# Attention over 64 keys: probabilities kept with the keys as rows, sums by TensorE, and keys and values made in the first layer

## What is computed

```python
x = x + per_token_matrix(layernorm(x), itok, ctx)      # row s is multiplied with a 256x256 matrix of ctx, chosen by itok[s]
x = x + top1_of_8_experts(layernorm(x), ...)            # 256 -> 512 -> 256, gelu
# third layer: q from layernorm(x), k and v from ctx, 16 heads of 16
scores = jnp.einsum('bhqd,bhkd->bhqk', q, k) * scale
scores = scores + mask * -1000000000.0
attn = jax.nn.softmax(scores, axis=-1)
ctx = jnp.einsum('bhqk,bhkd->bhqd', attn, v)
return jnp.einsum('bsd,ed->bse', ctx, Wo) + bo
x = x + gated_ffn_nvfp4(layernorm(x), ...)              # 256 -> 1024 -> 256, fake-quantized
```

## Time and profile before

| | |
|---|---|
| median of 3 runs | 788.87 us (785.74 to 792.18) |
| span of the profiled execution | 786.0 us |
| PE, DVE, ACT, POOL busy over the span | 78%, 74%, 51%, 27% |
| attention, 364 to 542 us: TensorE busy | 175.55 of 178 us |

### The profile page before, as it was taken

The page is one execution under the profiler, slowest core; times in us unless marked ns, Lnnn a source line. Parts: engine busy times, 40 slices in busy tenths (PEclk is TensorE's granted clock), DMA queues, the critical chain, the costliest instruction groups (busy, mean ns, idle before and its releaser), DMA issues.

```text
span 786.0 us, 14622 instructions
## 1 busy us (share of the span) xinstructions
PE 611.1 (78%) x4239; PEld 484.1 (62%) x4240; DVE 583.2 (74%) x1515; ACT 404.4 (51%) x780; POOL 209.1 (27%) x254
## 2 busy tenths in 40 slices
PE   5496786609899999958999999999744666766766
PEld 3384655409899898847888888887611433344424
DVE  6274666855645665667888889888648999999997
ACT  1341323003434233336565667665785798778762
POOL 5617363424644565510112222211100000000000
PEclk9698797858999999978999999999975799987998
DMA  8763242259375667261000000000000000000001
GB/s 321 228 209 118 71 137 76 96 181 385 107 232 173 185 197 230 78 185 34 1 0 0 0 0 0 0 1 1 2 3 1 0 27 27 13 27 13 27 27 54
DMA packets 35230, 68.22 MB, mean 87 GB/s; under 512 B 5405, under 2 KB 24238, under 8 KB 34160
## 3 DMA queue, kind: packets, MB, share of 16 engines
q1 hardware_dynamic: 28512, 52.20, 20.2%
q0 software_dynamic: 5520, 13.61, 5.1%
q10 hardware_dynamic: 1152, 1.88, 0.8%
HBM read 53.62 MB, written 15.80 MB: 88 GB/s over the span
## 4 chain that ended last, share of the span: by engine, by line
PE 36%; DVE 19%; issue 15%; ACT 13%; DMA 7%; another core or an unknown queue 3%; SPq 3%; POOL 2%; DVEq 1%; ACTq 0%; POOLq 0%
PE bank L1289 5%; PE quad L1162 4%; PE quad L1114 4%; PE quad L1273 3%; PE bank L1304 3%; PE bank L1171 3%; ACT hqT L1013 2%; DMA x_after_ffn<-row,niU 2%; PE quad L1454 2%; PE quad L1463 2%; ACT ctxs L996 2%; PE quad L1264 2%; DVE hh L2200 2%; DMA early<-in_W 2%
## 5 line engine op out<-in xcount | busy, mean ns | idle before, releaser
L746 ACT ACTIVATE hid<-quad,early 128x128 f32<-128x128 f32 x156 | 44.5, 368 | 87.8 <-PE quad L1162 86.5
L1162 PE MATMUL quad<-xts,early 128*128 128x128 f32 x624 | 76.5, 283 | 4.5 <-DMA early<-in_W 4.3
L1162 PEld LDWEIGHTS quad<-xts,early 128*128 128x128 f32 x624 | 74.9, 199 | 6.6 <-issue 5.5
L1171 PE MATMUL bank<-W2s,hid 128*128 x312 | 70.5, 379 | 0.0
L624 POOL TENSOR_TENSOR X<-fo,X 128x256 f32<-128x256 f32 (+1 forms) x32 | 21.8, 682 | 178.0 <-DVE fo L2046 178.0
L1289 PE MATMUL bank<-nVB,nPT 128*128 128x34 f32 x512 | 63.0, 279 | 0.0
L1171 PEld LDWEIGHTS bank<-W2s,hid 128*128 128x128 f32 x312 | 57.7, 190 | 7.1
L1289 PEld LDWEIGHTS bank<-nVB,nPT 128*128 128x128 f32 x512 | 59.6, 191 | 3.7
L1489 PE MATMUL bank<-dT,hqT 128*128 128x256 bf16 x224 | 41.0, 348 | 25.8 <-ACT hqT L1013 25.7
L577 POOL DMA_INDIRECT x_after_ffn<-row,niU x39 | 39.0, 1000 | 58.9 <-DVE row L1804 41.9
L1799 DVE SCALAR_TENSOR_TENSOR row<-bank,sco,row 128x256 f32<-128x256 f32 x39 | 18.5, 474 | 47.2 <-PE bank L1171 44.3
(11 more groups left out here) (325 smaller groups left out, 1431.6 us busy)
## 6 DMA issues: line engine op xcount, KB each, us to landing
early<-in_W SPq DMA_DIRECT2D x37, 514.0 KB
row<-rows_by_expert SPq DMA_DIRECT2D x38, 134.0 KB
...
```

Source lines behind the costliest of these rows:

```text
L746: ins = act.activation(hid[:, u, c * P:(c + 1) * P], bank[2 + u][:, c * P:(c + 1) * P], ACT.Gelu, bias=W1r[:, k, DC * H2 + c:DC * H2 + c + 1])
L1162: ins = pe.matmul(bank[2 + u][:, n * P:(n + 1) * P], W1r[:, m % RING, c * H2 + n * P:c * H2 + (n + 1) * P], xt[:, u, c, :], start=c == 0, ...
L1171: ins = pe.matmul(bank[6 + u % 2][:, 0:D], hid[:, u, c * P:(c + 1) * P], W2s[:, bass.ds(ex, 1), c, :].rearrange("p o s -> p (o s)"), start ...
```

## The change

The attention's arithmetic is arranged anew, in the branch that is run.

- **Mask and maxima.** `score` first writes the mask into `scored` by four bf16 matmuls (`onesb` x `maskb`) and adds the products on top. VectorE only takes the maxima out of PSUM (`row_max`). It splits them into three bf16 parts (`maxima`, four small operations), TensorE turns these (`maxima_turn`), ScalarE copies them (`maxima_out`).
- **Transposed scores.** `score_turned` computes the scores a second time with keys as rows and 256 queries as columns, into `keyed`, the other half of `quad`: c is a half of the heads. Four bf16 matmuls put in the negated maxima, four f32 matmuls add the products. ScalarE takes the exponential straight out of PSUM into `nPT` (`exps`), the key's mask being its bias.
- **Weighing.** `weigh` runs in four column tiles of 32, with `nVB` (values) and `sumb` (ones) as weights and 256 queries as columns, so that the weighted values and the sums both arrive in the two banks `duo` with features as rows. ScalarE inverts the sums by logarithm and exponential (`inverse_sums`), VectorE multiplies (`divide`), and `project` takes `nC` directly as weights: `probs_in`, `probs_out`, `project_turn` and their copies are gone.
- **Residual.** GpSimd adds the bias bo to the rows ahead of time (`biased`), VectorE adds the projection to them (`add_rows`).
- **Keys and values** are made in the first layer, two sequences at a time, after the `ranks` of a group, for eight groups (`keys_values`, `keys_values_out`), and kept in `Kall` and `Vall`. In attention GpSimd makes the key blocks from them (`keys_in`), ScalarE the value blocks (`values_in`). Wk, Wv and bk are loaded ahead of the other weights on SyncE. In the values each of two sequences goes to 64 rows of the output.
- **Around it.** Some 25 small VectorE operations after the routing prepare `maskb`, `selb`, `keym`, `sumb`, `rowb`. The loads of the last layer's weights (`wraw`) wait for the experts' first logits (`s_dl`). The transposes of those weights use one bank instead of two. On ScalarE the roots and the first rows of the last layer stand after the last batch.

The diff, cut to its core; "..." also stands for removed lines:

```diff
-        bank = [es.enter_context(nc.psum_tensor(f"bank{i}", [P, 512], F32)) for i in range(2)]
+        duo = es.enter_context(nc.psum_tensor("duo", [P, 2, 512], F32))
+        bank = [duo[:, i] for i in range(2)]
...
-        scored, turned = quad[:, :, 0:2 * P], quad[:, :, 2 * P:4 * P]
...
+            sp.dma_start(WkS[:], WkT).then_inc(s_kw, 16)
+            sp.dma_start(WvS[:], WvT).then_inc(s_kw, 16)
+            sp.dma_start(bkS[:], bk).then_inc(s_kw, 16)
             sp.dma_start(b2s[:], b2.rearrange("e h -> (e h)").partition_broadcast(P).rearrange("p (e h) -> p e h", e=E2)).then_inc(s_w, 16)
             sp.dma_start(WqS[:], WqT).then_inc(s_cw, 16)
...
+            sp.wait_ge(s_dl, 1)
...
+                def keys_in(p, b, h, first=False):
+                    if not first:
+                        pool.wait_ge(n_ST, b * 2 - 2)
                     pool.sem_inc(s_idle, 1)
...
+                    pool.tensor_tensor(nKB[h][:].rearrange("p c (t s) -> p c t s", t=2),
+                                       Kall[:, bass.ds(p, 1), :, h, :].rearrange("p o c s -> p (o c) s").unsqueeze(2).broadcast_to([P, DC, 2, KW]),
+                                       own2[:].unsqueeze(1).unsqueeze(3).broadcast_to([P, DC, 2, KW]), ALU.mult).then_inc(n_kb, 1)
+                def biased(b):
+                    pool.wait_ge(n_xn, b * 2 + 2)
+                    pool.sem_inc(s_idle, 1)
+                    xr = X2[:, bass.ds(b * 2 + 1, 2), 0:D]
+                    pool.tensor_tensor(xr, xr, boS[:].unsqueeze(1).broadcast_to([P, 2, D]), ALU.add).then_inc(n_xb, 1)
+                def batch(b, h, p, k=None):
+                    keys_in(p, b + 2, h)
+                    biased(b + 2)
                     if k is not None:
                         weight_scaled(k)
...
+            def keys_values_out(p):
+                act.wait_ge(s_kv, p + 1)
+                for n in range(DC):
+                    act.activation(Kall[:, p, n], bank[6][:, n * P:(n + 1) * P].rearrange("p (b s) -> p b s", b=2),
+                                   ACT.Identity, bias=bkS[:, n:n + 1])
+                act.copy(Vall[:, p], bank[6][:, D:2 * D]).then_inc(s_kve, 1)
...
+                def maxima_out(b):
+                    act.wait_ge(n_mT, b + 1)
+                    act.copy(nMT[:], bank[0].bitcast(BF16)[:, 0:S]).then_inc(n_mTe, 1)
+                def exps(b, c):
+                    act.wait_ge(n_ST, b * 2 + (c + 1))
+                    act.activation(nPT[c][:], keyed, ACT.Exp, bias=keym[:, 0:1]).then_inc(n_exp, 1)
...
+                def values_in(p, b, h, first=False):
                     if not first:
...
+                        act.wait_ge(n_W, b * 2 - 2)
+                    V4 = Vall[KW * h:KW * h + KW, bass.ds(p, 1), :].rearrange("s o (n t w) -> s (o n) t w", t=2, w=HD)
                     for t in range(2):
...
+                        ins = act.copy(nVB[h][KW * t:KW * t + KW, :, HD * t:HD * t + HD], V4[:, :, t, :])
                     ins.then_inc(n_va, 1)
...
+                def inverse_sums(b, c):
+                    act.wait_ge(n_W, b * 2 + (c + 1))
+                    act.activation(nR[:, c, :], duo[:, c, S:2 * S], ACT.Ln).then_inc(n_ln, 1)
+                    act.wait_ge(n_ln, b * 2 + (c + 1))
+                    act.activation(nR[:, c, :], nR[:, c, :], ACT.Exp, scale=-1.0).then_inc(n_rv, 1)
+                def batch(b, h, p=None, first=False, k=None, stage=0):
+                    exps(b, 0)
+                    if stage < 2:
                         queries_out(b + 1, 1 - h)
...
+                    exps(b, 1)
+                    if stage == 0:
+                        rows_out(b + 2)
+                    else:
+                        weights_out(0 if stage == 1 else 3)
+                    inverse_sums(b, 0)
+                    if stage < 2:
+                        values_in(p, b + 1, 1 - h, first)
+                    if stage == 0 and b is not NB - 3:
+                        rows_norm(b + 3)
+                    if stage:
+                        weights_out(1 if stage == 1 else 4)
+                    inverse_sums(b, 1)
                     if k is not None:
                         weight_half(k, first=isinstance(k, int) and k == 0)
...
+                    if stage < 2:
+                        maxima_out(b + 1)
+                    if stage:
+                        weights_out(2 if stage == 1 else 5)
...
+            def keys_values(p):
+                if p == 0:
+                    pe.wait_ge(s_kw, 16 * 3)
+                pe.wait_ge(s_kve, p)
+                rows = [ctxs[:, 2 * p:2 * p + 2, c, S - KW:S] for c in range(DC)]
+                for n in range(DC):
+                    for c in range(DC):
+                        pe.matmul(bank[6][:, n * P:(n + 1) * P], WkS[:, c, n * P:(n + 1) * P], rows[c], start=c == 0, stop=c == DC - 1)
+                for h in range(2):
+                    for c in range(DC):
+                        ins = pe.matmul(bank[6][KW * h:KW * h + KW, D:2 * D], ctxs[:, 2 * p + h, c, S - KW:S],
...
                 def score(b, h, q, first=False):
                     if q == 0:
                         pe.wait_ge(n_qe, b + 1)
                         pe.wait_ge(n_kb, b + 1)
...
+                        if not first:
+                            pe.wait_ge(n_exp, b * 2)
                     else:
...
+                        pe.wait_ge(n_rd, b * 2 + 1)
+                    for k, w in enumerate(tiles):
+                        pe.matmul(scored[:, k, :], onesb[w, :], maskb[w, :], start=True, stop=False)
                     for c in range(DC):
...
+                def maxima_turn(b, first=False):
+                    pe.wait_ge(n_mp, b + 1)
+                    if not first:
+                        pe.wait_ge(n_cn, b * 2)
+                    for q in range(2):
+                        ins = pe.transpose(bank[0].bitcast(BF16)[:, q * P:(q + 1) * P], nMb[:, q].rearrange("p k j -> p (k j)"), identb[:])
+                    ins.then_inc(n_mT, 1)
+                def score_turned(b, h, c):
+                    if c == 0:
+                        pe.wait_ge(n_mTe, b + 1)
+                        pe.wait_ge(n_rd, b * 2 + 2)
+                    else:
+                        pe.wait_ge(n_exp, b * 2 + 1)
+                    for k, w in enumerate(tiles):
+                        pe.matmul(keyed[:, k, :], selb[w, c * P:(c + 1) * P], nMT[w, :], start=True, stop=False)
+                    for k, w in enumerate(tiles):
+                        ins = pe.matmul(keyed[:, k, :], nKB[h][w, c, :], nQT[h][w, c, :], start=False, stop=True)
+                    ins.then_inc(n_ST, 1)
+                def weigh(b, h, c, first=False):
+                    pe.wait_ge(n_exp, b * 2 + (c + 1))
+                    if c == 0:
+                        pe.wait_ge(n_va, b + 1)
+                    if not first:
+                        pe.wait_ge(n_cn, b * 2 + (c - 1))
+                    for k, w in enumerate(tiles):
+                        pe.matmul(duo[w, c, 0:S], nVB[h][:, 4 * c + k, :], nPT[c][:, k, :], start=True, stop=True)
+                    for k, w in enumerate(tiles):
+                        ins = pe.matmul(duo[w, c, S:2 * S], sumb[:], nPT[c][:, k, :], start=True, stop=True)
+                    ins.then_inc(n_W, 1)
+                def project(b, q, first=False):
                     if q == 0:
...
+                        pe.wait_ge(n_cn, b * 2 + 2)
                     if first:
                         pe.wait_ge(n_fo, 1)
                     else:
...
+                        pe.wait_ge(n_ad, b * 2 + q)
                     for k in range(DC):
...
+                        ins = pe.matmul(bank[7][:, 0:D], nC[:, k, q * P:(q + 1) * P], WoS[:, k, :], start=k == 0, stop=k == DC - 1)
                     ins.then_inc(n_wo, 1)
...
+                def batch(b, h, first=False, stage=0):
+                    score_turned(b, h, 0)
                     if not first:
                         project(b - 1, 1)
...
+                    score_turned(b, h, 1)
+                    weigh(b, h, 0, first)
+                    if stage == 0:
+                        rows_in(b + 2)
+                    if stage == 1:
+                        pe.wait_ge(n_qe, NB)
+                    if stage:
+                        weights_in(0 if stage == 1 else 3)
+                    if stage < 2:
                         score(b + 1, 1 - h, 0)
...
+                    weigh(b, h, 1, first)
+                    if stage == 0:
+                        queries(b + 2, 0)
+                    else:
+                        weights_in(1 if stage == 1 else 4)
+                    if stage < 2:
+                        score(b + 1, 1 - h, 1)
+                    if stage == 0:
+                        queries(b + 2, 1)
+                    else:
+                        weights_in(2 if stage == 1 else 5)
+                    project(b, 0, first)
+                    if stage < 2:
+                        maxima_turn(b + 1)
...
```

(29 more changed lines are left out.)

477 lines of the change are left out of this document (165 added, 312 removed).

## The result

The changed kernel takes 2031.99 us (median of 4 runs, 2023.64 to 2035.81) where the kernel before takes 790.52: 2.57 times as long, 95% interval 2.56 to 2.58. The forecast of 793 us, with 778 to 810 as its range, is wrong, and no rival came near.

The account below looks back on a forecast made before the run. Attention was taken as bound by TensorE, with VectorE 11% behind, and the first layer by TensorE where undisturbed. Span 786.0 + 14 (keys and values) - 9.9 (attention) = 790, in runs 793 us, range 778 to 810.

Parts of the forecast that it names:

- no rival: Whole kernel: fast attention 779 (chance 0.24), clock 800 (0.2), first layer in full 801 to 808 (0.12), serial column tiles 845 (0.03).
- The forecast's largest loss: First layer, TensorE: 18 us of matmuls for keys and values, four fifths exposed, 14 us; bounds 7 and 22.
- The flag: After the routing, VectorE: some 25 small operations, 5 to 6 us, hidden in a 7.04 us wait; up to 5 if uncovered.
- The attention's pace: Attention loop: a chain through three engines plus 0.3 for the clock gives 12.0 us a batch instead of 12.7.
- the walk: Attention, one batch followed from first exponential to the next through TensorE, ScalarE and VectorE: durations and hand-overs sum to 11.7 us.
- the forecast 0.94: Attention loop: TensorE's granted clock, taken between 0.99 and the last layer's 0.85; counted as 0.3 us a batch.
- Gain over 14 batches: Attention: 14 x (12.7 - 12.0) = 9.9 us saved, bounds 0 and 22.
- the ends: Start and end of attention: no change counted, with 3 us either way at the end for the range.
- TensorE's forms: Attention: new scores, transposed scores and weighing priced from rows; TensorE's work per batch 8.7 us instead of 12.7.
- Column tiles together: Attention's weighing: a half's 16 records run four tiles at once, 0.95 us, rather than 3.5 one after another.
- Its busy share in the loop: Attention loop: TensorE busy about 75% instead of 99%.
- The sum: Whole kernel: profiled span 786.0 + 14 - 9.9 = 790, in runs 793, 0.5% slower; no real change, chance 0.41.

Follow-up runs that it names:

- e3: The repaired kernel (e1) without TensorE's matmuls for keys and values in groups 2 to 8 of the first layer: 782.18 us, ratio to before 0.9995.
- e9: The kernel before with the rows of groups 4 to 9 of the first layer loaded by SyncE's plain transfers: 762.71 us, ratio to before 0.968.
- e1: The changed kernel with the flag repaired (mask's spread added, not taken as maximum) and the score's accumulation closed once: 782.68 us, ratio to before 0.990.
- e4: e1 with second division behind the maxima, their transpose before projection, second half's score before queries, weights' rounding before the residual: 763.05 us, ratio to before 0.975.
- e2: The kernel before with one operation more, raising the mask's bound to at least 0 so that its own general branch runs: 2029.48 us, ratio 2.571.

## Why the first layer took nothing (e3, e6, e9, e10)

The forecast's largest loss, 14 us for keys and values, did not come: in e1 VectorE starts on the experts' rows at 169.34 instead of 175.48. The blocks are there, at the cheap price (1.07 us to the next start, and 1.02):

```profile
89.99 1.14 PE L1138 MATMUL bank<-ctxs,WkS 128*128 128x128 f32 x8
91.06 1.09 PE L1141 MATMUL bank<-WvS,ctxs 128*64 128x256 f32 x8
92.08 1.18 PE L1114 MATMUL quad<-ctxs,xts 128*128 x4
```

In the stretch 66 to 124 TensorE is busy 49.05 us where it was 37.77: 11.3 us more work in the same time. First the work was taken out of the repaired kernel (e3), and useless work put into the old one (e6).

```diff
                 pe.wait_ge(s_kve, p)
+                if p:
+                    pe.sem_inc(s_kv, 1)
+                    return
```

> The repaired kernel with TensorE's matmuls for keys and values left out in groups 2 to 8 of the first layer (only those of the first pair are made; ScalarE copies the same block eight times), so the attention computes with wrong keys but does the same work. Theory S (the first layer between 66 and 124 us is not bound by TensorE, and its unnamed waits shrink when TensorE brings more work between the groups): the first layer ends as late as in the kernel before or later, VectorE's first work on the experts' rows at about 175 instead of 169.3, and the long waits of 66 to 82 and 113 to 124 are back; the total is the same as of the repaired kernel or up to 6 us more, 783 to 789. Rival T (my prediction's term: TensorE's 2.2 us a group are exposed at four fifths): 12 us less, 770.

```diff
+                if 0 < g <= NB // 2:
+                    for n in range(2):
+                        for c in range(DC):
+                            pe.matmul(bank[6][:, n * D:(n + 1) * D], ctxs[:, 2 * g - 2, c, 0:P], ctxs[:, 2 * g - 1, c, 0:S],
+                                      start=c == 0, stop=c == DC - 1)
```

> The kernel before with useless work added on TensorE in the first layer: four f32 matmuls of 128x256 into a bank that nobody reads, behind the routing of groups 1 to 8, about 1.75 us each time, 14 us in all. Theory S: the routing ends no later, or up to 6 us earlier; 784 to 790. Rival T: 11 us more, 802.

Measured: e3 782.18 us, half a microsecond from e1 (which was timed on another chip; ratio to before 0.9995, 0.995 to 1.004); its first work on the experts is at 171.7, its stretch 66 to 124 has TensorE at 40.93 busy. e6 786.32 us, ratio 0.9992 (0.995 to 1.004), TensorE at 46.19. The work costs nothing that can be measured in either kernel: rival T, my prediction's term, falls. That it would even shorten the stage is not shown: 171.7 against 169.34 is one execution each, and the totals don't differ. (Held against the kernel before on their own chips, e3 stands at 0.9995 and e1 at 0.990; by neither measure is anything gained by taking the work out.)

Two things in the traces make room for it. One is slack. In e1 GpSimd's runs of eight transfers (four rows' scatters, four gathers) start like this:

```profile
71.73 1.02 POOL L563 DMA_INDIRECT rows_by_expert<-row,pi  x1 [3.60 <-DVE pi L1683]
...
85.26 1.02 POOL L563 DMA_INDIRECT rows_by_expert<-row,pi  x1 [3.52 <-DVE pi L1683]
...
98.93 1.02 POOL L563 DMA_INDIRECT rows_by_expert<-row,pi  x1 [3.66 <-DVE pi L1683]
```

So a group comes every 13.6 us, of which GpSimd issues for 10 and waits 3.6 for VectorE's positions, while TensorE's own work on a group, keys and values included, is 10.8 us (the period that it keeps in e10 below). The other is the clock. Behind its two long waits the kernel before makes its products slowly:

```profile
83.75 6.97 PE L1114 MATMUL quad<-ctxs,hid 128*128 x16 [1.68 <-ACT hid L684]
```

It happens again at 125.86 (6.40 us); otherwise 16 products take 3.8 to 4.4 us there, and in e1, with short waits, no unbroken 16 take more than 3.94. So some 5 to 6 us of the block's 17 are paid back in this way; the granted clock of the stretch 66 to 124 is 0.82 in the kernel before and in e3, 0.88 in e6 and 1.00 in e1.

What bounds the stage, then? GpSimd issues 8 indirect transfers per group at about 1.3 us each, and in the kernel before TensorE, VectorE and ScalarE had waited together, ScalarE for something without a name. In e9 six of ten groups get their rows by SyncE's plain transfers; e10 does the same to e1.

```diff
                 sp.wait_ge(s_x1, 2 * e + 2)
+                if e + NXG < NG:
+                    for u in range(count1(e + NXG)):
+                        r = (4 * (e + NXG) + u) * P % NT
+                        sp.dma_start(xg[e % NXG][:, u, :], x[r:r + P, :]).then_inc(s_gat2[e % NXG], 16)
...
-                if g + NXG < NG:
-                    pool.wait_ge(s_x1, 2 * g + 2)
-                    gather(g + NXG)
...
```

> The kernel before; the rows of groups 4 to 9 of the first layer are loaded by SyncE's ordinary transfers from consecutive addresses instead of GpSimd's indirect ones (so these are other rows than the index asks for; all else is computed as before). GpSimd then issues 4 indirect transfers per group (5.2 us) instead of runs of 8 and more. Theory P (the long waits on three engines at once at 66 to 82 and 113 to 124 come with GpSimd's uninterrupted runs of indirect transfers): the waits are gone, the routing ends 10 us or more earlier, total 774 to 780. Rival Q (they come from the first use of code or from the transfers' traffic): the waits stay, the routing ends within 3 us of now.

> The repaired kernel (e1) with the same plain transfers for the rows of groups 4 to 9 as in e9 (other rows than the index asks for). The blocks for keys and values take 2.15 us of TensorE in each of eight groups, 17 us. Theory P (they are free only because GpSimd's indirect transfers keep TensorE waiting): with the transfers halved they come out, and the last ranks end at 132 (e9) + 17 = 149, against 151.2 in e1; total near 779. Rival (they fit into other waits of TensorE, as for VectorE): the last ranks end near 132 to 138, total 762 or less.

Measured: e9 762.71 us, ratio to before 0.968 (0.960 to 0.976), more than the 774 to 780 of theory P; e10 771.85, ratio 0.981 (0.971 to 0.990), its last ranks at 140.7, between the two theories (149 and 132 to 138). The stretch 66 to 124 of e9, then of e10:

```profile
66.00:124.00 58.00, 54.08 (x321) 42.06 (x321) 49.77 (x288) 20.04 (x54) 23.69 (x24) 1.00 0.44 140
```

```profile
66.00:124.00 58.00, 58.00 (x373) 46.83 (x373) 45.51 (x257) 24.06 (x69) 19.79 (x20) 1.00 0.41 131
```

Without the gathers on GpSimd the long waits are gone: TensorE is busy 54.08 of 58 us instead of 37.77, and the last `ranks` come at 132.0 instead of 156.8, 24.8 us earlier. So GpSimd's gathers bounded this stage: by their number, by the length of the runs, or by the wait that stands ahead of each gather in GpSimd's order and went out with it; these two kernels don't tell these apart. How they hold up TensorE, VectorE and ScalarE at once the profile doesn't say. Both kernels work on other rows than the index asks for; what follows takes about as long all the same (from the last ranks to the bounds' transpose 177.7 us in e9, 180.6 in the kernel before). And with that bound gone keys and values do cost something: TensorE is busy 58.00 of 58, the last ranks are 8.7 us later than in e9, and the total is 9.1 us higher (on another chip). That is half of the 17 us of work: the groups of e10 come 10.8 us apart, and those of e9 9.8, not the 8.7 of TensorE's work alone. What paces e9 was not tested; VectorE, 49.8 of 58 us busy, is the likely one.

## Which chain sets the pace (e5, e8, e4, e7)

In e1 the second maximum of a batch waits behind the second division, which waits for ScalarE's second inversion:

```profile
373.45 0.41 DVE L2075 TENSOR_TENSOR nC<-duo,nR 128x256 f32<-128x256 f32 x1
375.28 0.42 DVE L2075 TENSOR_TENSOR nC<-duo,nR 128x256 f32<-128x256 f32 x1 [1.42 <-ACT nR L880]
375.63 1.22 DVE L2061 TENSOR_REDUCE nM<-quad 128x16 f32<-128x1024 f32 x1
```

**e5_divide_late** moves that division behind the maxima, and the maxima's transpose ahead of the projection:

```diff
                     divide(b, 0)
-                    divide(b, 1)
                     row_max(b + 1, 1)
                     maxima(b + 1)
+                    divide(b, 1)
...
-                        pe.wait_ge(n_cn, b * 2)
+                        pe.wait_ge(n_cn, b * 2 - 1)
...
-                    project(b, 0, first)
                     if stage < 2:
                         maxima_turn(b + 1)
+                    project(b, 0, first)
```

> The repaired kernel with the second division of a batch behind the next batch's maxima on VectorE, and the maxima's transpose ahead of the projection on TensorE. In the trace the second maximum waits for the second division although its scores end at 374.97 (batch 1), and it starts at 375.63. Theory W (the chain of a batch goes through that division): the pace falls by 0.5 to 0.7 us a batch, 7 to 10 us in all, to 773-776. Rival C2 (the clock or ScalarE sets the pace): no change.

Measured: 788.10 us, ratio to before 1.003 (0.999 to 1.007), no gain. The second maximum starts earlier (6.96 us behind the batch's first exponential instead of 7.55), but the projection now stands between the maxima's transpose and the next transposed score, and ScalarE waits 1.43 us for that one instead of 0.94: without weights the pace is 11.3, with them 14.2.

On top of e5, **e8_score_ahead** moves the second half's score (the first two pieces below), and **e4_reordered** the rounding of weights as well (`between`):

```diff
                     weigh(b, h, 1, first)
+                    if stage < 2:
+                        score(b + 1, 1 - h, 1)
                     if stage == 0:
                         queries(b + 2, 0)
...
-                    if stage < 2:
-                        score(b + 1, 1 - h, 1)
...
+                    if between:
+                        between()
                     if not first:
                         add_rows(b - 1, 1)
                         new_stats(b - 1, 1)
-                    if between:
-                        between()
                     row_max(b + 1, 0)
```

> As e5 (divide late), with the second half's score ahead of the queries on TensorE, but VectorE's rounding of weights where it was, between the residual and the first maximum; so it differs from e4 by that alone. Theory W1 (the score's place is what matters; e5 failed because its second maximum still waited for the score behind a query): near e4, 763 to 768. Rival W2 (the rounding's place does it, since it delays the first maximum in the batches with weights): 775 or more, with 13 to 14 us a batch where weights are rounded.

> As the one before, with the second half's score ahead of the queries on TensorE, and VectorE's rounding of weights ahead of the previous batch's residual. Theory W: the second maximum can then start at the end of the first one plus 0.8, about 374.3 instead of 375.63; the pace without weights falls from 11.4 to about 10.2, the total by 14 to 18 us, to 765-769. Rival C2: no change, or less than 4 us since another chain (ScalarE's two inversions) is as long.

Measured: e8 773.83 us, ratio 0.982 (0.976 to 0.988). e4 763.05 us, ratio 0.975 (0.964 to 0.986), by medians 23 us under the kernel before on its chip and 19.6 under e1 on another (by the ratios to the kernel before, 0.975 against e1's 0.990, the step is 1.5%, and the intervals just meet). The profiles carry it: e4's attention is 24 us shorter than e1's in the table above. ScalarE's timeline of e4, the first exponential of two batches with weights:

```profile
452.66 1.11 ACT L866 ACTIVATE nPT<-quad,keym 128x1024 f32<-128x1024 f32 x1 [1.43 <-PE quad L1293]
...
463.35 1.11 ACT L866 ACTIVATE nPT<-quad,keym 128x1024 f32<-128x1024 f32 x1 [1.43 <-PE quad L1293]
```

10.69 us, and 10.7 in 12 of the 14 steps from batch 1 to batch 15. The score's place makes 10.7 of 11.4 where there are no weights (in e8 too); the rounding's place makes 10.7 of 12.4 to 13.4 where there are. VectorE's rounding in e8, then in e4:

```profile
446.90 0.77 DVE L2049 TENSOR_SCALAR ctxs<-ctxs 128x768 f16<-128x768 f16 x1
447.71 1.23 DVE L2050 TENSOR_SCALAR ctxs<-ctxs 128x768 int16<-128x768 int16 x1
...
449.75 1.22 DVE L2061 TENSOR_REDUCE nM<-quad 128x16 f32<-128x1024 f32 x1
```

```profile
453.07 0.34 DVE L2049 TENSOR_SCALAR ctxs<-ctxs 128x768 f16<-128x768 f16 x1
453.45 0.36 DVE L2050 TENSOR_SCALAR ctxs<-ctxs 128x768 int16<-128x768 int16 x1
```

In e8 it lies under GpSimd's work on keys and bias (446.85 to 448.7) and takes 0.77 and 1.23 us instead of 0.34 and 0.36, and the first maximum starts late behind it. The Trainium skill (GPSIMD Engine Reference, Specifications) says that GpSimd shares its SBUF interfaces with VectorE and that the two contend on instructions in a 2-port mode or with two SBUF inputs; that the same lines are slow beside GpSimd and fast without it agrees with this, though the profile doesn't show in which mode they run. The stretch 362 to 500 us in e4, then in e8, then the last layer in e4 (the last column but two is the granted clock):

```profile
362.00:500.00 138.00, 126.22 (x1510) 76.16 (x1514) 84.97 (x197) 94.40 (x187) 36.76 (x42) 1.00 0.00 0
```

```profile
362.00:500.00 138.00, 115.36 (x1356) 69.03 (x1354) 90.72 (x178) 84.69 (x166) 35.12 (x40) 0.99 0.00 0
```

```profile
539.50:758.50 219.00, 138.72 (x824) 78.34 (x832) 187.60 (x289) 156.31 (x200) 0.00 (x0) 0.80 0.06 20
```

In attention both keep the full clock, where e1 has 0.94 over the same stretch. Shorter waits don't explain that: between 425 and 505 us TensorE waits up to 0.4 us ahead of the maxima's transpose in e4, but up to 1.7 in e8, as in e1. What does was not tested.

**e7_two_buffers** goes on from e4: `nC` in two buffers, both projections of a batch in the next batch, weights scaled earlier on ScalarE. TensorE's part, without its conditions:

```diff
                     score_turned(b, h, 0)
-                    if not first:
-                        project(b - 1, 1)
+                    project(b - 1, 0, 1 - h)
                     score_turned(b, h, 1)
                     weigh(b, h, 0, first)
+                    score(b + 1, 1 - h, 0)
+                    weigh(b, h, 1, first)
                     rows_in(b + 2)
-                    score(b + 1, 1 - h, 0)
-                    weigh(b, h, 1, first)
                     score(b + 1, 1 - h, 1)
+                    project(b - 1, 1, 1 - h)
                     queries(b + 2, 0)
                     queries(b + 2, 1)
                     maxima_turn(b + 1)
-                    project(b, 0, first)
```

> As e4, with the chain cut further: nC in two buffers, both projections of a batch in the next batch (the first beside the first exponential, the second behind the second score), the first score right behind the second exponential, and on ScalarE the inversion of the first sums and the scaling of weights right behind the exponentials. Walked with e4's durations: exponential 1.0, transposed score 0.75, exponential 1.1, score 0.75, maximum 1.3, score 0.75, maximum 1.3, split 0.9, transpose 0.3, copy 0.4, transposed score 0.75, hand-overs: 9.6 us a batch where e4 has 10.7; 15 batches, 16 us, so 747. Rival: ScalarE or TensorE (busy 8.7 us of it) becomes the bound at 10.2 or more, 755 to 763.

Measured: 762.90 us, ratio 0.968 (0.962 to 0.974), no faster than e4. The pace is 10.4 without weights and 10.9 with them; I had walked 9.6. TensorE now has a projection and two queries between the second score and the maxima's transpose, 2.6 us, and reaches the transpose 0.5 us after the maxima are ready; with weights the rounding runs into the first maximum again. The gain of one wait is the next one's start.

## The prediction, step by step

- **The flag: the step that failed.** "VectorE gets some 25 small operations after the routing, 5 to 6 us at 0.19 to 0.35." I priced these operations and did not compute what they write. One of them sets the value that chooses the branch, and no rival said that the new code might not run, though the whole diff, not the cut shown above, had all that it takes. Every other term of the sum is a term of a branch that never ran. The maximum with 0 or 1e30 (L1754) put the program on its general branch, where attention takes 1481 us instead of 236; e1 and e2 show it from both sides. The time of the small operations was priced well: in e1 they run from 163.1 to 167.8 and are hidden.
- **Keys and values: "four fifths of 18 as exposed: 14 us; bounds 7 and 22."** Wrong in kind. "TensorE is the bound there where the stage runs undisturbed" was read from two groups at the stage's start, when GpSimd's first run of 16 transfers (58.92 to 79.19) had hardly begun. The 20 us in which TensorE stood idle were the better row: the stage had another bound, and what fits under it costs nothing. The price of a block was right at its low end (2.1 us).
- **The attention's pace: 12.0, bounds 11.15 to 12.7.** Measured 12.33 in e1. The chain was the right one (inversion, division, second maximum, split, transpose, copy), at 11.3 to 11.5 where the walk had 11.7. Missing was the term for the weights, 0.5 to 2.8 us in eight batches: the dear small operations beside GpSimd, and the clock. That its mean came out at the forecast 0.94 is luck: it was reckoned for every batch alike, and it is 1.00 in those without weights and lower in the others. Gain over 14 batches 5.2 us instead of 9.9, and 1.6 lost at the ends.
- **TensorE's forms.** Column tiles together: right. Its busy share in the loop was forecast at 75% and is 84% (149.20 of 178). The low clock is not the reason: from 379.40 to 402.19, at a clock of 1.00, it is 19.58 of 22.79 us, 9.8 us a batch where the prediction adds up 8.7. From start to start the two pieces of the queries take 1.06 and 0.99 us where 1.73 was counted for both, and the rows' transposes 0.59 instead of 0.44; the changes of shape between short pieces were counted too low.
- **The sum.** 790 was forecast for the span of a kernel that runs its new branch, 781.5 measured: 20.6 us less up to the bounds' transpose (14 more forecast, 6.6 less measured), 6.3 more in attention, and 5.7 more in the last layer, where nothing was forecast. So the repaired kernel's 783 us lie inside the range of 778 to 810 by terms that cancel, not by the working. The 6.6 us are not the work on keys and values, which e3 leaves out: its bounds' transpose stands at 331.4. In the seven profiles with the changed first layer and all gathers (the changed kernel, e1, e3, e4, e5, e7, e8) it stands at 330.2 to 333.4, in the kernel before, e2 and e6 at 333.8 to 337.4; whether and by what the change shortens it was not tested.
